# Outputs of rows 24 to 31 of a recurrence: whole rows on GpSimd and VectorE, or columns on GpSimd and TensorE

## The reference

```
def step(Sst, inp):
    qt, kt, vt, bt, gt = inp
    Sd = gt[..., None, None] * Sst
    kS = jnp.einsum('bhk,bhkv->bhv', kt, Sd)
    Snew = Sd + jnp.einsum('bhk,bhv->bhkv', kt, bt[..., None] * (vt - kS))
    ot = jnp.einsum('bhk,bhkv->bhv', qt, Snew)
    return (Snew, ot)
...
o = _rmsnorm(o, out_norm_w) * jax.nn.silu(gate)
return o.reshape(b, s, d) @ out_proj_W.T + out_proj_b
```

## Time and profile before

| what | value |
|---|---|
| median of 3 runs | 885.64 us (885.04 to 885.79) |
| profiled execution, its own time | 881.1 us |
| span of the profiled execution | 879.4 us |
| mean granted TensorE clock | 0.977 |
| TensorE busy with matmuls | 793.7 us (90%) |
| VectorE busy | 614.7 us (70%) |
| ScalarE busy | 391.3 us (45%) |
| GpSimd busy | 183.5 us (21%) |

### The profile page before, as it was taken

How to read it: one execution, slowest core, us unless ns; L and a number is a source line. 1 busy time by engine, 2 the same in 40 slices (tenths; PEclk the granted TensorE clock), 3 DMA queues, 4 the chain that set the end, 5 groups by cost and what they waited for, 6 DMA issues and landing times.

```text
span 879.4 us, 19821 instructions
## 1 busy us (share of the span) xinstructions
PE 793.7 (90%) x7700; PEld 586.2 (67%) x7700; DVE 614.7 (70%) x976; ACT 391.3 (45%) x561; POOL 183.5 (21%) x197
## 2 busy tenths in 40 slices
PE   4998978989986988977798998799999999999997
PEld 3665757944543666755487885477777777777775
DVE  5796697678787386898767977767777655545544
ACT  5344764610224143666457965334444432323332
POOL 7000790006999801000402420000000000000000
PEclk9999979999999999999999999799999999999999
DMA  8000000020000000010130001144444322222221
GB/s 310 1 2 1 3 1 3 3 96 1 0 0 1 0 2 1 1 39 1 37 78 14 22 21 38 57 127 158 154 150 154 109 68 57 70 69 69 68 61 51
DMA packets 24073, 46.07 MB, mean 52 GB/s; under 512 B 2605, under 2 KB 10541, under 8 KB 23629
## 3 DMA queue, kind: packets, MB, share of 16 engines
q1 hardware_dynamic: 24013, 45.21, 16.8%
HBM read 41.91 MB, written 1.36 MB: 49 GB/s over the span
## 4 chain that ended last, share of the span: by engine, by line
PE 70%; DVE 21%; ACT 4%; issue 3%; POOL 1%; DMA 1%; SPq 0%; DVEq 0%; ACTq 0%; POOLq 0%
PE psum L1790 11%; PE psum L1791 11%; PE psum L1792 11%; PE psum L1982 6%; PE psum L1992 4%; PE psum L828 4%; PE psum L829 4%; PE psum L830 4%; PE psum L2124 1%; DVE arena L1460 1%; PE psum L2170 1%; DVE arena L1658 1%; PE psum L1963 1%; PE psum L2187 1%; PE psum L2156 1%
## 5 line engine op out<-in xcount | busy, mean ns | idle before, releaser
L1790 PE MATMUL psum<-xh,arena 128*128 128x296 f16 (+1 forms) x664 | 193.3, 291 | 8.3 <-DVE xl L1333 5.0
L1791 PE MATMUL psum<-xl,arena 128*128 128x296 f16 (+1 forms) x664 | 193.2, 291 | 0.0
L1792 PE MATMUL psum<-xh,arena 128*128 128x296 f16 (+1 forms) x664 | 193.2, 291 | 0.0
L697 DVE TENSOR_TENSOR arena<-arena 128x592 f16<-128x592 f32 x68 | 52.7, 775 | 61.1 <-ACT arena L608 60.8
L603 ACT ACTIVATE arena<-psum 128x592 f32<-128x592 f32 x66 | 43.8, 664 | 115.7 <-PE psum L1792 115.7
L1790 PEld LDWEIGHTS psum<-xh,arena 128*128 (+2 forms) x664 | 65.3, 98 | 30.8 <-DVE xl L1333 4.5
L752 DVE TENSOR_TENSOR arena<-psum,arena 128x592 f32<-128x592 f32 x64 | 49.6, 775 | 50.8 <-PE psum L1792 50.6
L828 PE MATMUL psum<-arena 128*128 128x296 f16 x272 | 79.9, 294 | 4.6 <-DVE arena L697 3.8
L608 ACT ACTIVATE arena<-arena 128x592 f16<-128x592 f32 x66 | 46.0, 696 | 77.6 <-DVE arena L691 74.8
L829 PE MATMUL psum<-arena 128*128 128x296 f16 x272 | 79.9, 294 | 0.0
L830 PE MATMUL psum<-arena 128*128 128x296 f16 x272 | 79.8, 293 | 0.0
(11 more groups left out here) (321 smaller groups left out, 1675.3 us busy)
## 6 DMA issues: line engine op xcount, KB each, us to landing
arena<-comb SPq DMA_DIRECT2D x62, 296.0 KB, 3.3
arena<-in_wmoe SPq DMA_DIRECT2D x34, 384.0 KB, 3.0
arena<-in_xt SPq DMA_DIRECT2D x4, 864.0 KB, 9.6
arena<-in_w SPq DMA_DIRECT2D x2, 1024.0 KB, 6.6
arena<-arena SPq DMA_DIRECT2D x6, 187.0 KB
arena<-in_ctrl SPq DMA_DIRECT2D x1, 1056.0 KB, 9.1
out<-arena SPq DMA_DIRECT2D x2, 512.0 KB, 3.1
arena<-in_wlin SPq DMA_DIRECT2D x1, 768.0 KB, 4.4
```

The costliest lines, as they stand in the source:

```text
L697: dve.tensor_tensor(al[:, s_], t1, ah[:, s_], ALU.subtract).then_inc(ev["al"], 1)
L1790: pe.matmul(dst, wh, mh, start=start, stop=False)
L1791: pe.matmul(dst, wh, ml, start=False, stop=False)
L1792: return pe.matmul(dst, wl, mh, start=False, stop=stop)
```

## The change

QGROUPS loses group 3, so QROWS, the width of the columns and the split of the tail all move from 24 to 32. Rows 24 to 31 are made as whole rows; columns keep only rows 32 to 36, 5 x 64 = 320 elements. The square at QROWS + 4 moves from step 28 to step 36. As one PSUM tile fewer has a number, all later tiles move down by one bank, and the holders of the two banks into which the last norm's sums 2 and 3 are moved are now looked up: they become the reciprocal sum 0 of the same norm (bank 0) and its variance (bank 7).

```diff
-QGROUPS = [3, 4]
+QGROUPS = [4]
 QROWS = GROUPS[QGROUPS[0]][0]
 OPARTS = [0, QROWS, S]
 QWIDE = 64 * (S - QROWS)
...
+        def last_in(b):
+            return [key for key in order[:place[("ln4", "r", 2)][0]] if place[key][0] % 8 == b][-1]
+
         n0 = place[("f2", 0, 0)][0]
...
-                 ("ln4", "r", 2): (0, ("ln4", "v")), ("ln4", "r", 3): (7, ("ln4", "m", 3))}
+                 ("ln4", "r", 2): (0, last_in(0)), ("ln4", "r", 3): (7, last_in(7))}
```

## The result

The changed kernel takes 893.78 us (median, 890.54 to 895.85) beside 885.34 us for the kernel before in the same session: a ratio of 1.0092, 95% interval 1.0060 to 1.0124. That is 8.4 us slower. Slower was forecast, by 4.9 us; the measured median lies 0.2 us past the upper end of the range.

What follows compares the result with a forecast made beforehand. GpSimd was taken to bound the recurrence from step 20; the tail starts 4.9 us later, so the profiled 881.1 becomes 886.0, and 4.5 us from profiled execution to median gives 890.5 us, range 887.6 to 893.6.

Steps and rivals of the forecast that it cites:

- (a): Steps 8 to 15: TensorE keeps up with VectorE, so step 16 starts at 238.0 in place of 243.40, 5.4 us won.
- (b): Steps 16 to 19: VectorE works without waits; row 17's reduce ends at 249.4 and releases GpSimd's row product 19 at 249.5.
- (c): From row product 19 GpSimd is the bound: row products 19 to 31 and columns take 56.5 us, ending at 306.0.
- rival 2: GpSimd doesn't bound; VectorE paces steps 24 to 33, which end at 293 in place of 308.3: 875 us, chance 0.05.
- (d): VectorE's reduce of row 31 waits for 306.0, ends at 308.3; step 36's copy at 310.1 in place of 303.36.
- (e): The tail of square, sum, root and multiplies: first turned-back output at 319.3 against 314.35, so 4.9 us later.
- The column path: TensorE's last output columns near the recurrence's end: no longer late, last adds end by 312.
- the table load: ScalarE's 1.28 us load before the square root: covered by a wait, put at nothing, up to 1.3 us if not.
- Rival 1: TensorE's clock stays low into the tail; turning and projections at half speed, +2 to +3 us, 893; chance 0.14.
- The prediction's last sign of error: The forecast is wrong if the stages behind 325 us change in length.
- Rival 3: GpSimd's unbroken run starts some 3 us sooner, at row product 16: 885.6 to 887.4 us, chance 0.10.
- The moved banks: Last norm's third reciprocal sum now takes bank 0, covered by VectorE's work: put at nothing, up to 0.5 us otherwise.

Runs made afterwards that it cites:

- after: The changed kernel's first run and profile, beside the kernel before: 893.78 us, ratio 1.0092; its profiled execution took 890.54 us.
- again: The changed kernel run once more without an edit: 891.11 us, ratio 1.0097 to the kernel before.
- narrow: Changed kernel with row products and reduces of rows 24 to 31 cut to 8 columns, the rest of the sums left out: 868.90 us, 0.9842.
- warm: Changed kernel with 10 filler matmuls in each of steps 22 to 33 and 44 in place of 24 ahead of the turning: 887.66 us, 1.0045.
- fillers: Changed kernel with 44 filler matmuls in place of 24 ahead of the turning: 889.16 us, ratio 1.0086 to the kernel before.
- pad: Changed kernel with one unused tile number, so every later PSUM tile keeps its bank from before: 891.45 us, 1.0110.
- old: The kernel before the change, run again without an edit: 884.77 us, ratio 1.0008.
- oldwarm: Kernel before the change with 10 filler matmuls in each of steps 23 to 25 and 34 in place of 24 ahead of the turning: 883.02 us, 1.0009.
- oldtable: oldwarm with the square root's table loaded by ScalarE ahead of its last copies: 882.72 us, ratio 1.0004 to the kernel before.
- tailwarm: Changed kernel with rows 0 to 23 squared and summed early, 10 fillers in each of steps 24 to 33, 44 ahead of the turning: 889.75 us, 1.0079.

## Why the prediction was right and where it fell short

**(a), right.** Step 16 at 238.0 was forecast, and 237.54 came, with step 8 itself 0.8 us earlier than in the profile of before. From step 8 to step 16 it takes 25.00 us, forecast 24.67, before 30.07. TensorE adds eight columns of outputs in these steps, so it is spared 8 x 0.86 = 6.9 us, and 5.1 us of that reach step 16.

**(b), right in its time only.** Row product 19 was to start at 249.5, released by the reduce of row 17, and started at 249.14. But nothing released it: GpSimd is full from row product 17 on (242.68), and row product 19 stands behind GpSimd's own column (248.43). That the two times agree is luck.

**(c), right.** From row product 19 to the end of row product 31 56.5 us were forecast, and 56.3 came in after (249.14 to 305.44) and in again. The price on the line, 4.27 us, was met exactly in after; again has 4.22. The Trainium skill (GPSIMD Engine Reference, section 3.1) gives 4497 ns for a two-input operation of this width, an add; the trace has 4.27 us for this multiply, and the measurement decides. That GpSimd bounds is shown by narrow, not only by its full row: 20 us taken off its products moved their end by 19.3. That closes rival 2, which would have had the time at 875.

**(d), right for VectorE:** from the end of row product 31 to the last copy 4.07 us, forecast 4.1. That the copy came at 309.51 against 310.1 is less telling: after had step 8 at +26.48, 1.7 us earlier than the profile that the forecast was built on. Counted from row 0 with the same step 8, again has it at +125.13, forecast 124.95. The square takes 1.89 us against 1.9, the sum starts when it ends.

**The end of (d) and (e), the step that failed:** "The column path is no longer late: its last adds end by 312", the table load that "I put at nothing", and the first turned-back output at 319.3. The forecast had the last adds end 1.9 us behind the last copy's start; it is 2.67 us in after and 3.12 in again. These prices were taken at TensorE's full clock, though the prediction itself had the clock at 1.2 GHz in steps 24 to 31 and called it hidden under GpSimd. It is hidden up to the last row product; from there on TensorE is on the path. Against the forecast, counted from the copy of row 0 in the profile of before, again's gate is late by 2.1 us (136.23 against 319.3 - 185.15 = 134.15), in these terms:

- 0.2 in the recurrence (125.13 against 124.95);
- 0.7 from step 36's copy to the reciprocal (5.67 against a forecast of 5.0): the adds at low clock delay ScalarE's copy of the last columns and the table load behind it, and the root waits. With the clock up (warm) it is 5.11. In after it was 5.22, so this term differs by execution;
- 1.2 from the reciprocal to the gate (5.43 against 4.2). Of that 0.8 is the clock in the turning, since fillers has 4.60 (0.5 if pad's 5.12 is taken for again's 5.43). The remaining 0.4 stands at full clock too: the last multiply is 320 elements in 0.49 us where 832 took 1.02. The turning of the first banks starts behind the multiply ahead of it and lay beside these two; I had put it at nothing without naming that cover. In fillers, at full clock, the gate still waits 0.49 us for the turning; the reading was not tried by itself.

Rival 1, the low clock in the turning, thus came true at a chance of 0.14, with 0.8 us at the gate's start and 1.3 at its end in place of 2 to 3; it belonged into the forecast. The kernel before pays the same price in some executions (old, above), so it isn't all a cost of the change. The Trainium skill (TensorE: Matmul & The Clock Gate, section on HAM oscillation) says that work alternating with waits is throttled again and again. The trace agrees: in after the clock falls to 0.50 and comes back three times between 266 and 312 us, with 0.74 and 0.66 as the means of 260 to 280 and 280 to 300. "The fillers end within 2 to 3 us of the turning, as today" held in its number (2.78 us between them) and not in its conclusion.

**What is left.** From +7.5 or +7.6 at the gate's end to +8.4 on the medians there is about 1 us in later stages. By the last column of the table these took 559.3 to 564.2 us. That goes with the granted clock from 200 to 300 us behind the gate's end: 0.95 to 0.97 in the six profiles with 559.3 to 560.6 us, 0.91 to 0.93 in the eight with 561.6 to 564.2, oldwarm and oldtable among them. With the changed kernel's work (after to tailwarm, eight profiles) the mean is 562.5, with that of before (four profiles) 561.0. The two groups overlap, and again and pad lie 3.4 us apart on the same engines' work. So a shift of 1 to 2 us behind the gate is possible and not shown; it stays open. The prediction's last sign of error, a change of length behind 325 us, was no good sign, as they come with edits that leave those stages alone too (fillers 559.3, oldtable 562.0 us); the two pairs with the same code lie within 0.2 us of each other.

Rival 3 had GpSimd's unbroken run start earlier, at row product 16. It did start earlier than I derived, at 17, but row product 19 came no earlier than forecast, so its 3 us were not given back. The moved banks, put at nothing, are at nothing by pad.

**A better version?** Not found. With the turning at full clock in both (warm and oldwarm), the change still costs 6.1 us at the gate's end (139.83 against 133.75), 5.1 us with the split tail as well. With the clock at 1.00 through the end of the recurrence in both (warm and oldtable), it costs 7.4 us at step 36 (125.19 against 117.79). So most of the loss isn't the clock's. Of the kernels measured, the kernel before, with or without help, is the fastest of those that do the full work.

## What to carry to other kernels

Work taken off the engine that makes others wait pays only as far as the next engine has room: here TensorE gave 5.1 us in steps 8 to 15, and from step 16 to 36 GpSimd, without a gap for 60 us, took back 12.0 (71.96 us in again, 59.96 before; 13.7 by after and old). Look behind the moved work too. An engine left with little to do may lose its clock, at no cost while it is hidden and at a price in the first dependent step behind; and where two paths end together, shortening one of them shows nothing until both are cut. Effects of 1 to 3 us in a program whose whole time scatters by 5 are read between landmarks of a profile, and a gain seen only there, as in tailwarm, isn't yet a faster kernel.

## What was unexpected in the hardware

- With the same code, the recurrence's first eight steps took 26.5 or 28.2 us, by a dip of TensorE's granted clock, and the stages behind the gate, in which at most the banks differ, took 559.3 to 564.2 us. In again the slower executions have the lower mean clock (888.90 us at 0.953, 893.49 us at 0.946); in oldwarm they need not (881.59 us at 0.970, 884.12 us at 0.977).
- The table load of 1.28 us can be moved by one tiny operation that uses the same function earlier (oldtable): the gate comes 0.8 us sooner.
- GpSimd's 2048-wide product of two fp32 operands takes 4.22 to 4.27 us, on the line of the narrow ones; a 320-wide column of outputs takes 0.74 to 0.80 us.
